# Products with V in four column groups of the TensorE array instead of three

## What is computed

```
att = einsum('bqhd,bkhd->bhqk', q, k) * scale
att = where(causal, att, -inf)
att = softmax(att, axis=-1)
out = einsum('bhqk,bkhd->bqhd', att, v)
```

## Time and profile before

| | us |
|---|---|
| median of three runs | 4648.91 |
| lowest and highest of the three | 4644.92, 6351.21 |
| profiled execution | 4640.95 |
| its span, first to last instruction | 4639.2 |
| granted TensorE clock, mean | 0.978 |

### The profile page before, as it was taken

The page is one execution under the profiler, slowest core; times in us unless marked ns, Lnnn a source line. Parts: engine busy times, 40 slices in busy tenths (PEclk is TensorE's granted clock), DMA queues, the critical chain, the costliest instruction groups (busy, mean ns, idle before and its releaser), DMA issues.

```text
span 4639.2 us, 114644 instructions
## 1 busy us (share of the span) xinstructions
PE 4074.3 (88%) x39208; PEld 2969.3 (64%) x39208; DVE 3330.0 (72%) x6327; ACT 2692.9 (58%) x5901; POOL 363.6 (8%) x374
## 2 busy tenths in 40 slices
PE   6999888879999888999988879999888999888888
PEld 4667665566766646667665656767646667665665
DVE  5777776767777767777776767777767777776776
ACT  2555556556665655555556555656655555556555
POOL 1000002000000110000002000000110000002000
...
GB/s 70 36 36 36 42 36 28 0 49 36 48 50 36 36 0 42 36 36 36 42 36 28 0 49 36 52 47 36 36 0 42 36 36 36 42 36 28 0 42 42
DMA packets 48635, 160.95 MB, mean 35 GB/s; under 512 B 12420, under 2 KB 12934, under 8 KB 48006
## 3 DMA queue, kind: packets, MB, share of 16 engines
...
...
## 4 chain that ended last, share of the span: by engine, by line
PE 62%; DVE 15%; issue 14%; ACT 4%; POOL 2%; DVEq 1%; DMA 1%; ACTq 0%; SPq 0%; POOLq 0%
PE PT L683 10%; PE OUT L703 10%; PE S L669 5%; PE PT L801 5%; PE S L728 4%; DVE nmax L1203 4%; DVE work L378 4%; PE S L627 2%; PE FR L627 2%; PE S L772 2%; PE FR L575 2%; PE S L575 2%; DVE XT L1074 2%; PE FR L634 1%; PE S L634 1%
## 5 line engine op out<-in xcount | busy, mean ns | idle before, releaser
L926 ACT ACTIVATE work<-S,nmax 128x256 f32<-128x256 f32 (+7 forms) x1536 | 1138.7, 742 | 1123.6 <-DVE nmax L1203 1059.3
L1203 DVE TENSOR_REDUCE nmax<-S 128x1 f32<-128x256 f32 (+7 forms) x1536 | 1157.6, 754 | 801.1 <-PE S L671 781.3
L683 PE MATMUL PT<-ident,work 128*128 128x128 f32 x6912 | 1103.3, 280 | 222.9 <-DVE work L378 195.1
L683 PEld LDWEIGHTS PT<-ident,work 128*128 128x128 f32 x6912 | 745.1, 142 | 430.7 <-DVE work L378 259.2
L378 DVE COPY work<-PT 128x512 f32<-128x512 f32 (+3 forms) x1536 | 894.4, 582 | 41.6 <-PE PT L683 35.4
L669 PE MATMUL S<-KS,QS 128*128 128x512 f16 (+3 forms) x1152 | 321.9, 334 | 61.6 <-ACT work L926 28.7
L671 PE MATMUL S<-causal,identb 128*128 128x128 bf16 x1536 | 339.1, 221 | 0.0
L669 PE MATMUL S<-odd 128*128 128x512 f16 (+3 forms) x1152 | 315.7, 328 | 23.0 <-ACT work L926 21.6
L930 ACT ACTIVATE work<-PT 128x512 f32<-128x512 f32 (+3 forms) x768 | 331.2, 431 | 3.4 <-PE PT L683 3.4
L703 PE MATMUL OUT<-work,odd 128*32 128x128 f32 x6912 | 304.9, 277 | 0.0
L1237 DVE TENSOR_REDUCE gm<-S 128x1024 f32 (+1 forms) x180 | 220.1, 1223 | 117.4 <-PE S L772 117.1
...
## 6 DMA issues: line engine op xcount, KB each, us to landing
...
odd<-hi_z SPq DMA_DIRECT2D x128, 192.0 KB, 4.2
odd<-odd SPq DMA_DIRECT2D x128, 192.0 KB, 4.2
...
QS<-hi_z SPq DMA_DIRECT2D x64, 192.0 KB, 4.0
QS<-odd SPq DMA_DIRECT2D x64, 192.0 KB, 4.1
KS<-hi_z SPq DMA_DIRECT2D x64, 192.0 KB, 4.3
KS<-odd SPq DMA_DIRECT2D x64, 192.0 KB, 4.5
```

The source lines that it names most:

```text
L683: last = tr(bank[:, P * (j - c0):P * (j - c0) + P], PS[m % 2][:, m // 2 % 2, P * j:P * j + P], ident[:, :])
L926: A(PS[n % 2][:, n // 2 % 2, 0:w], S[:, n % 2, 0:w], ACT.Exp, bias=nmax[:, n % MAXES:n % MAXES + 1], accum_out=rowsum[:, sum_col(n):sum_co ...
L1203: v.tensor_reduce(nmax[:, n % MAXES:n % MAXES + 1], S[:, n % 2, 0:P * (qtile(n) + 1)], AX.X, ALU.max, negate=True).then_inc(max_made, 1)
```

## The change

Four units share a burst, a quad. In units 0 to 31 of an image they are heads 0 to 3 of one query tile. In units 32 to 47 they are heads 4 and 5 of two query tiles (`PAIRS`: tiles 0 and 1, 6 and 7, 2 and 3, 4 and 5); there a round beyond the smaller tile's blocks has two products. The fourth head or tile goes to partitions 96 to 127 of OUT. An image has 12 quads and three batches of four quads. The burst of a small quad stands at slot 8 (k // 2) + 10, where it stood within its slot; that of a large quad at 8 (k // 2) + 12, and now ahead of the slot's transposes. The copy of OUT is in slot 16 j + 21, its transposes (now 128 partitions) and `add_to_t1` in slot 16 j + 22. The order of heads and tiles over the slots changes with it, and `stacked[1]` is waited for before slot 6. The count of PT banks' uses is now kept per group of images.

```diff
@@ -46,17 +46,18 @@
 
 
 UNITS = NH * TT
-KI = UNITS // 3
+KI = UNITS // 4
+PAIRS = [((0, 1), (6, 7)), ((2, 3), (4, 5))]
-PV_AT = (8, 11)
+PV_AT = (10, 12)
 BATCH = 4
 NBI = KI // BATCH
 SUMS = 4
 MAXES = 16
-OT_AT, BACK_AT = 18, 19
+OT_AT, BACK_AT = 21, 22
...
+def head_and_tile(n):
+
+    block, at, large = n % UNITS // 8, n % 8 // 2, n % 2
+    if block < 4:
+        return at, TILES[block][large]
+    return 4 + at % 2, PAIRS[block - 4][large][at // 2]
+
+
 def qtile(n):
-    return TILES[n // 6 % 4][n % 2]
-
-
-def triple_of(n):
-    return 2 * (n // 6) + n % 2
+    return head_and_tile(n)[1]
+
+
+def quad_of(n):
+    return 2 * (n // 8) + n % 2
 
 
 def unit_of(k, hh):
-    return 6 * (k // 2) + k % 2 + 2 * hh
+    return 8 * (k // 2) + k % 2 + 2 * hh
 
 
 def last_slot(images):
-    return 12 * (NBI * images - 1) + BACK_AT
-
-
-def triples_at(images, slot):
-
-    return [k for k in range(KI * images) if 6 * (k // 2) + PV_AT[k % 2] == slot]
+    return 16 * (NBI * images - 1) + BACK_AT
+
+
+def quads_at(images, slot, parity):
+
+    return [k for k in range(parity, KI * images, 2) if 8 * (k // 2) + PV_AT[parity] == slot]
 
 
 def batches_at(images, slot, at):
 
-    return [j for j in range(NBI * images) if 12 * j + at == slot]
+    return [j for j in range(NBI * images) if 16 * j + at == slot]
 
 
 def batch_tiles(j):
@@ -103,8 +112,8 @@
 
 def sum_col(n):
 
-    k = triple_of(n)
-    return 3 * (BATCH * (k // BATCH % SUMS) + place(k)) + n % 6 // 2
+    k = quad_of(n)
+    return 4 * (BATCH * (k // BATCH % SUMS) + place(k)) + n % 8 // 2
 
 
 def transposed(images):
@@ -120,8 +129,8 @@
...
-        oT = sb("oT", [CH, BATCH * P])
-        rowsum = sb("rowsum", [P, 3 * BATCH * SUMS])
+        oT = sb("oT", [P, BATCH * P])
+        rowsum = sb("rowsum", [P, 4 * BATCH * SUMS])
...
-                eng.wait_ge(pv_made, after(g, 0, KI, triple_of(m - 2 * RING) + 1))
+                eng.wait_ge(pv_made, after(g, 0, KI, quad_of(m - 2 * RING) + 1))
...
+            def times_v(g, images, k):
+                u, units = k // KI, [unit_of(k, hh) for hh in range(4)]
+                done = [i for i, c in enumerate(CHUNKS[images]) if c[1] == "p" and c[2] <= units[3]]
+                for b in range(2):
+
+                    pe.wait_ge(pt_free[b], g * PT_GROUP + (max(i for i in done if i % 2 == b) // 2 + 1))
+                if k % KI == 0:
+
+                    for step in STEPS[-2:]:
+                        wait_freed(pe, g, u, step)
+                if k and k % BATCH == 0:
+
+                    pe.wait_ge(oT_made, after(g, 0, NBI, k // BATCH))
+                o = P * place(k)
+                for j in range(max(qtile(m) for m in units) + 1):
+                    for hh, m in enumerate(units):
+                        h, qt = head_and_tile(m)
+                        if j <= qt:
+                            last = mm(OUT[32 * hh:32 * hh + 32, o:o + P], V[u % 2][:, j, D * h:D * h + D],
+                                      PTS[k % 2][:, m // 2 % RING, P * j:P * j + P],
+                                      start=(j == 0), stop=(j == qt), tile_position=(0, 32 * hh))
+                last.then_inc(pv_made, 1)
+
...
-                        u, h, qt = n // UNITS, 3 * (n % UNITS // 24) + n % 6 // 2, qtile(n)
-                        if n % 24 == 0:
-
-                            pe.wait_ge(stacked[n % UNITS // 24], after(g, u, STACKS, STACKS))
+                        u, (h, qt) = n // UNITS, head_and_tile(n)
+                        if n % UNITS in (0, 6):
+
+                            pe.wait_ge(stacked[h // 3], after(g, u, STACKS, STACKS))
...
+                    if quads_at(images, n, 1):
+                        times_v(g, images, quads_at(images, n, 1)[0])
...
-                    for k in triples_at(images, n):
...
+                    if quads_at(images, n, 0):
+                        times_v(g, images, quads_at(images, n, 0)[0])
...
                             for q in range(BATCH):
-                                last = tr(PT[i % 2][:, CH * q:CH * q + CH], oT[:, P * q:P * q + P],
-                                          ident[0:CH, 0:CH])
+                                last = tr(PT[i % 2][:, P * q:P * q + P], oT[:, P * q:P * q + P], ident[:, :])
...
-                        A(oT[:, :], OUT[0:CH, :], ACT.Copy).then_inc(oT_made, 1)
+                        A(oT[:, :], OUT[:, :], ACT.Copy).then_inc(oT_made, 1)
...
-                n = 3 * BATCH
-                u, grp, qts = j // NBI, j % NBI // 2, batch_tiles(j)
-                ts, cols = slice(qts[0], qts[-1] + 1, 2), slice(CH * grp, CH * grp + CH)
+                dve.wait_ge(pt_full[i % 2], g * PT_GROUP + (i // 2 + 1))
+                n = 4 * BATCH
+                u, qts = j // NBI, batch_tiles(j)
+                if j % NBI < 2:
+                    ts, cols, nt, nh = slice(qts[0], qts[-1] + 1, 2), slice(0, 4 * D), 4, 4
+                else:
+                    ts, cols, nt, nh = slice(0, TT), slice(4 * D, C), TT, 2
                 t1 = T1[:, u, ts, cols]
                 v.reciprocal(rsums[:, :], rowsum[:, n * (j % SUMS):n * (j % SUMS) + n]).then_inc(t1_step, 1)
                 dve.wait_ge(t1_step, base + 1)
-                v.tensor_tensor(t1.rearrange("p t (h d) -> p t h d", h=3),
-                                PT[i % 2][:, 0:BATCH * CH].rearrange("p (t h d) -> p t h d", t=BATCH, h=3),
-                                rsums[:, :].rearrange("p (t h) -> p t h", t=BATCH).unsqueeze(3).broadcast_to(
-                                    [P, BATCH, 3, D]), ALU.mult).then_inc(t1_step, 1)
+                v.tensor_tensor(t1.rearrange("p t (h d) -> p t h d", h=nh),
+                                PT[i % 2][:, :].rearrange("p (t h d) -> p t h d", t=nt, h=nh),
+                                rsums[:, :].rearrange("p (t h) -> p t h", t=nt).unsqueeze(3).broadcast_to(
+                                    [P, nt, nh, D]), ALU.mult).then_inc(t1_step, 1)
                 dve.wait_ge(t1_step, base + 2)
                 dve.sem_inc(pt_free[i % 2], 1)
                 v.tensor_tensor(t1, t1, T0[:, u % 2, ts, cols], ALU.add).then_inc(t1_step, 1)
```

More of the change, by code:

```diff
@@ L122 @@
 CHUNKS = {images: transposed(images) for images in (2, GROUP)}
-PT_IMG = len(CHUNKS[2]) // 4
-assert all(len(c) == 2 * PT_IMG * images for images, c in CHUNKS.items())
+PT_GROUP = len(CHUNKS[GROUP]) // 2
+assert len(CHUNKS[GROUP]) == 2 * PT_GROUP
 STEPS = ["xt0", "xt1", "xt2", "xt3", "g0", "g1", "wg0", "wg1", "na", "rb", "u", "mt", "t0", "t1", "t2", "t3",
@@ L679, in attention @@
                             if i >= 2:
-                                pe.wait_ge(pt_free[i % 2], after(g, 0, PT_IMG, i // 2))
+                                pe.wait_ge(pt_free[i % 2], g * PT_GROUP + i // 2)
                             for j in range(c0, c0 + k):
@@ L923, in attention @@
                             i = max(i for i, c in enumerate(CHUNKS[images]) if c[1] == "p" and c[2] == n - 4)
[L924 removed]
+                            act.wait_ge(pt_full[i % 2], g * PT_GROUP + (i // 2 + 1))
                         w = P * (qtile(n) + 1)
```

24 lines of the change are left out of this document (2 added, 22 removed).

## The result

| | before | after |
|---|---|---|
| median of the runs, us | 4646.91 | 4726.17 |
| lowest and highest, us | 4644.13, 6351.21 | 4723.67, 4790.53 |
| span of the profiled execution, us | 4639.2 | 4723.9 |
| granted TensorE clock, mean | 0.978 | 0.964 |

The ratio is 1.0207, 95% interval 1.0166 to 1.0249; by the medians it is 1.017, slower by 79 us, where 135 us less had been forecast. The ratio leaves out before's 6351.21, one disturbed execution, but has in it after's 4790.53, an execution at a granted clock of 0.914. That the kernel got slower is clear; whether by more than 2% is not.

The account below looks back on a forecast made before the run. PE was taken to set the time except in slots 12 to 17 (neither engine full) and 24 to 30 (DVE). Terms -5.1 + 2.1 - 0.9 - 0.4 = -4.3 us an image led to 4512 us, range 4465 to 4600.

Parts of the forecast that it names:

- The forecast's times 32: The sum of -4.3 us an image times 32 gave -138 us; plus 3 for the ends, -135 us.
- (a): Products with V: 16 bursts, 72 rounds become 12 and 56; four-group pass 0.109 us; PE 4.69 us less an image.
- Rival 3: Fourth column group not concurrent: a pass takes 0.218 us, an image 7.5 us longer, 4890 us; chance 0.08.
- (b): Where the bursts lie: their PE-bound part falls from 15.4 to 10.3 us an image, 5.1 less; the rest is hidden.
- (c): Slots 12 to 17 get longer through DVE's larger tiles and its wait behind slot 12's burst: 14.2 us, 2.1 more.
- (d): Slots 24 to 30 get shorter: 0.9 us less DVE maxima, about 0.4 less for the moved ScalarE copy of OUT.
- (e): Three output batches instead of four, in PE-bound slots: small changes in PE, DVE and ScalarE work, taken as 0.
- the ring PTS: Ring of four transposed tiles, emptied by one burst: each copy waits for the burst before it; nothing added.
- (f): New order of work, including tighter copies for large bursts: 0, with 1 us an image as the upper end.
- The early need of heads 3 to 5: Heads 3 to 5 needed in slot 6 instead of 24; DMAs land with 5 us of margin, cost 0.
- 2 (DVE's waits eat half): DVE waits at transposes, slots 1 to 4 and 45 to 47, give back 2.3 us an image; 4585 us, chance 0.17.
- The sign that I gave for it: Image shrinks by under 3 us with (a) right, and the transposes' idle time grows from 222.9 us.

Follow-up runs that it names:

- s1: The kernel before the change with 16 of 72 rounds an image left out of its bursts: 4578.7 us, ratio to before 0.9862.
- s2: e3 with 16 rounds an image put back as repeated products, result unchanged: 4716.1 us, ratio to before 1.0159.
- e2: The changed kernel with the large quad's burst a slot earlier, in slot 11 behind that slot's transposes: 4717.5 us, ratio to before 1.0167.
- e1: The changed kernel with the transposes of oT and add_to_t1 a slot later (22, 23 instead of 21, 22): 4689.7 us, ratio to before 1.009.
- o1: e3 with the order of tile pairs turned round, so slots 24 to 31 get (1,7): 4606.7 us, ratio to before 0.9913.
- e3: The changed kernel with the edits of e1 and e2 together: 4629.2 us, ratio to before 0.9978.
- b1: o1 plus seven extra matmuls in slots 15 to 17, and each image's middle batch two slots later: 4577.2 us, ratio to before 0.9856.
- b2: b1 with PAIRS turned round, so heads 4 and 5 do tiles 2 to 5 first: 4597.8 us, ratio to before 0.99.
- d1: The changed kernel with two extra matmuls, result unused, in each of slots 24 to 30: 4710.1 us, ratio to before 1.014.
- h2: The kernel before the change with the large triple's burst ahead of its slot's transposes instead of behind: 4632.9 us, ratio to before 0.998.

## Why the prediction was wrong

Sum for an image: forecast -4.3 us. Measured +3.46 (106.58 to 110.04) in the 20 inner images, which is 1.82 fall-free and 1.64 more of falls. The forecast's times 32 does not hold: of the 85 us by which the profiled span grew, these 20 have 69, the first images of the six groups 15, the last ones 5, and the rest is 5 shorter.

- **(a) Rounds and bursts: right.** A pass over four groups takes what one over three did (64 loads in 1.69 us, 48 in 1.68). Rival 3 is out. The Trainium skill's table of tilings in "TensorEngine Tiling (Array Packing)", Available Configurations, holds here; the bus bug that the Trainium skill notes in "TensorE: Matmul & The Clock Gate", step 1, does not show in these matmuls, and the trace decides.
- **(b) What arrives of them: nearly right for the rounds.** The forecast had 5.1 us of PE-bound work go, its 16 rounds (3.5 us) and the fixed costs together; s1 and s2 show 2.9 to 3.1 us for the 16 rounds. The fixed cost of four bursts was not measured alone.
- **(c) Slots 12 to 17: right.** 14.2 forecast, 13.73 measured; DVE's work rose to 10.29 us as forecast (10.3). Its idle time behind the burst and at the reciprocal was forecast as 2.0 and 1.7 us and is 1.87 and 1.28 (the reciprocal is now L1130):

```profile
1228.07 0.69 DVE L387 COPY work<-PT 128x512 f32<-128x512 f32 x1 [1.87 <-PE PT L717]
...
1238.62 0.16 DVE L1130 RECIPROCAL sc<-sc 96x2 f32<-96x2 f32 x1 [1.28 <-ACT RD L868]
```

e2 shows that this is mostly the burst's place: moved to slot 11 it makes 12-17 shorter by 1.95 and 0-11 longer by 1.62.
- **(d) Slots 24 to 30: wrong.** About 12 forecast, 13.67 measured. DVE's work did fall, by 0.5 us (13.41 to 12.92), but DVE waited 0.8 us in it; with the batch a slot later (e1) it is 13.11. The forecast also took 0.9 us off the stretch for the pair (2,4) in place of (1,7); o1, which puts (1,7) back, takes only 0.19 us more than e3 (13.36 against 13.17).
- **(e) The batches: the step that failed.** I took 0 because PE's and DVE's own work hardly changes. What changed is the parity of the slot, 19 to 22: behind two uses of the two banks instead of one. e1 and e3 price it at 2.3 to 2.4 us an image, 75 us if all 32 images pay alike. The forecast asked what a copy waits for at the ring PTS, and did not ask it of the two banks PT, whose queue is three long in these slots.
- **(f) The new order of work: the second failure.** It was taken at 0 with 1 us as its upper end; s2 gives 1.4 to 2.6. That range holds the tiles of (c), all of (d) and the batches as well, which the forecast had at +1.3 - 0.9 - 0.4 + 0 = 0, so it is the new order as a whole that is priced, not (f) by itself. The stretch that grew most is 36-40: 12.98 us in e3 against 11.76, though a burst of 1.17 us has left. Part of this is work that moved in, since these slots now have the units of tiles 1 and 7 and a batch (DVE busy 11.11 us against 9.03, PE 12.11 against 11.77). The batch's place there accounts for 0.44 net (b1), the order of the pairs for none (b2 takes 0.3 us out and puts 0.5 into 41-47). What the rest is stays open. The early need of heads 3 to 5 cost nothing that the trace shows: PE waits once for a DMA ahead of scores, 6.5 us, and once, 6.3 us, in the kernel before.
- **The clock: not in the forecast at all.** It took 1.64 us an image, 33 us in the 20 inner images (52 if all 32 pay alike). The forecast itself moved PE work out of the DVE stretch and called that free. The PE time of slots 24 to 30 went from 9.89 to 8.77 us, and the clock fell there or just behind in nearly every image; with that time raised to 11.47 us (d1) it falls in half of them. The rule was at hand: the Trainium skill's page "TensorE: Matmul & The Clock Gate", Part 1, ties the granted clock to how busy the engine has been, and the trace agrees (d1 against after).

Of the rivals, 2 (DVE's waits eat half) named the right kind of mechanism, with the wrong place (slots 1 to 4, 45 to 47) and a third of the size. The sign that I gave for it, more idle time ahead of the transposes, came true and misleads: e3 has that idle time and not the loss. No rival on the slower side was the one that came.

Of the 7.8 us by which the sum for an image missed, the banks are 2.4 and the clock 1.6. The other 3.7 are the new order, the large bursts' slots and what did not arrive of the 5.1, which the runs separate only in part.

The account closes: -3.0 (16 rounds) -1.2 (four bursts, at most) +2.6 (order, at most) = -1.6, which is e3 against before; +2.4 (banks), +1.1 (the large burst's slot), +1.6 (clock) = +3.5, the 3.46 measured. The first sum closes by construction, since the order is what the 16 rounds and the bursts leave; that the banks cost the same in e1 (2.3) as in e3 (2.4) is the independent part. That the burst's slot costs 1.1 us here and nothing in h2 I can only argue: more than half of it comes from the burst of slot 36 (1.38 less in 36-40, 0.74 more in 31-35 in e2), which stood among the products of Q and K; in the kernel before no large burst stood in slots 36 to 40.
